# One-core gated cross-attention block: maxima of the first heads, weight preparation and token tiles moved to other steps

## What is computed

```python
x = x + tanh(g_xattn[0]) * mha(layernorm(x), ctx, ctx)        # 16 heads, causal from column 1089 on
h = layernorm(x)
# every row is scaled by its own maximum, then rounded to fp8
qx, sx = fp8_rows(h);  g = qx*sx @ (fp8_rows(Wgate)).T;  u = qx*sx @ (fp8_rows(Wup)).T
t = silu(g) * u                                               # 1408 hidden features
qt, st = fp8_rows(t);  y = qt*st @ (fp8_rows(Wdown)).T
x = x + tanh(g_ffn[0]) * y
```

## Time and profile before

| | us |
|---|---|
| median of 3 runs | 1055.09 |
| lowest, highest | 1054.97, 1057.81 |
| the profiled execution, own time | 1050.76 |
| its span in the trace | 1049.0 |
| PE, DVE, ACT, POOL busy | 952.6, 843.5, 684.4, 313.7 |

### The profile page before, as it was taken

One profiled execution on the slowest core, in us unless ns is written; L12 is line 12 of the kernel. 1 busy time (PEld: TensorE's weight loads), 2 busy tenths in 40 slices (PEclk: granted clock), 3 DMA queues, 4 the chain that ended last, 5 costly groups with the idle time before them and its releaser, 6 DMA issues.

```text
span 1049.0 us, 21140 instructions
## 1 busy us (share of the span) xinstructions
PE 952.6 (91%) x7706; PEld 396.1 (38%) x7706; DVE 843.5 (80%) x1438; ACT 684.4 (65%) x1420; POOL 313.7 (30%) x335
## 2 busy tenths in 40 slices
PE   3588899999999999999999999999999999989565
PEld 2223333333333434443434433444434343434333
DVE  7888988888987888787788979787888878645687
ACT  2047576777767776767667767777666766667544
POOL 3011333333321423232323324141323233334223
PEclk9999999999999999999999999999999999889889
DMA  6893342232792212123942221216832020000001
GB/s 135 124 215 93 78 118 67 67 95 62 166 125 55 81 46 60 43 64 92 127 85 58 59 72 33 69 38 137 116 61 64 11 48 27 1 11 2 11 2 41
DMA packets 157231, 74.89 MB, mean 71 GB/s; under 512 B 111096, under 2 KB 142920, under 8 KB 157128
## 3 DMA queue, kind: packets, MB, share of 16 engines
q1 hardware_dynamic: 155240, 67.70, 30.6%
q0 software_dynamic: 1760, 5.77, 2.1%
q10 hardware_dynamic: 128, 0.07, 0.0%
HBM read 43.28 MB, written 4.19 MB: 45 GB/s over the span
## 4 chain that ended last, share of the span: by engine, by line
PE 67%; DVE 18%; issue 7%; ACT 5%; POOL 2%; ACTq 0%; DVEq 0%; POOLq 0%
PE ps L963 22%; PE ps L937 14%; PE ps L880 8%; DVE mch L1193 7%; PE ps L984 6%; PE ps L1007 3%; PE ps L867 2%; PE ps L885 2%; ACT pr L692 2%; DVE ff L1100 1%; PE ps L906 1%; PE ps L943 1%; PE ps L918 1%; DVE ff L1093 1%; PE ps L908 1%
## 5 line engine op out<-in xcount | busy, mean ns | idle before, releaser
L692 ACT ACTIVATE pr<-ps 128x512 f32<-128x512 f32 (+4 forms) x832 | 398.3, 533 | 141.5 <-PE ps L937 84.3
L1193 DVE TENSOR_REDUCE mch<-ps 128x2 f32<-128x1024 f32 (+4 forms) x416 | 432.9, 1055 | 45.6 <-PE ps L885 23.4
L963 PE MATMUL ps<-pr,vf 128*33 128x512 f32 (+4 forms) x1664 | 378.3, 534 | 0.0
L937 PE MATMUL ps<-qst,kst 97*64 97x512 f16 (+4 forms) x1600 | 252.2, 371 | 12.7 <-ACT pr L692 9.2
L880 PE MATMUL ps<-kTh,qTh 32*128 32x512 f16 (+4 forms) x832 | 154.9, 370 | 21.9 <-DVE mch L1193 19.7
L880 PEld LDWEIGHTS ps<-kTh,qTh 32*128 32x128 f16 x832 | 39.6, 92 | 266.5 <-issue 115.2
L937 PEld LDWEIGHTS ps<-qst,kst 97*64 97x64 f16 (+1 forms) x1600 | 78.0, 110 | 106.3 <-ACT pr L692 67.4
L963 PEld LDWEIGHTS ps<-pr,vf 128*33 128x33 f32 (+1 forms) x1664 | 86.3, 112 | 55.1 <-issue 3.7
L1282 DVE SCALAR_TENSOR_TENSOR ff<-ps,scs,wsb 128x352 f32<-128x352 f32 x56 | 32.4, 582 | 56.0 <-PE ps L984 56.0
L984 PE MATMUL ps<-wgu,t_T 128*64 128x352 bf16 x768 | 66.5, 316 | 0.0
L486 POOL TENSOR_TENSOR ff<-ff,wsb 128x352 f32<-128x352 f32 x48 | 45.4, 946 | 67.0 <-DVE ff L1282 67.0
(11 more groups left out here) (157 smaller groups left out, 1163.4 us busy)
## 6 DMA issues: line engine op xcount, KB each, us to landing
kst<-kTh SPq DMA_DIRECT2D x128, 100.1 KB, 2.2
ksrc<-in_ctx SPq DMA_DIRECT2D x16, 768.0 KB
vf<-in_ctx SPq DMA_DIRECT2D x48, 256.0 KB, 5.6
kst<-kTl SPq DMA_DIRECT2D x64, 100.1 KB, 2.2
xs<-in_x SPq DMA_DIRECT2D x16, 256.0 KB, 4.1
qst<-qTh SPq DMA_DIRECT2D x128, 32.0 KB, 1.9
near<-in_ctx SPq DMA_DIRECT2D x4, 1024.0 KB, 7.8
out<-xs SPq DMA_DIRECT2D x16, 256.0 KB, 2.0
```

The lines of the kernel that those rows point to most:

```text
L692: nc.scalar.activation(pr[0:kn, n % NP, q0:S], ps[0:kn, j, q0:S], ACT.Exp, scale=SCALE).then_inc(ex_done, 1)
L937: last = nc.tensor.matmul(ps[a:e, j, q0:S], kst[s][0:ST, r, k0 + a:k0 + e], qst[s][0:ST, r, q0:S], start=True, stop=(t < DT))
L963: nc.tensor.matmul(ps[64 * j:64 * j + VW, 2 + pp % 2, q0:S], vf[0:kn, t, h, :], pr[0:kn, n % NP, q0:S], start=(t == 0), stop=(t == NT - 1) ...
L1193: nc.vector.tensor_reduce(mch[:, qt, 2 * hp:2 * hp + 2, c], both[:, :, 0:k1 - k0], AX.X, ALU.max).then_inc(dve_free, 1)
```

## The change

Six things are changed.

1. Only the first pair's 13 maxima jobs (`HALF`) of group 0 are made ahead of the loop, and its row of shifts is finished and sent alone (`first_finish`, `first_shift`). The other 13 jobs of group 0, all 26 of group 1 and 6 of group 2 are spread over the first 26 steps by `first_until`, up to two in one step.
2. Staging of group 0 uses PSUM banks of its own for three of its five parts (`FIRST_BANKS`), the gate matmul stands behind it on PE, ACT loads its function table with a dummy instruction, and the two memsets of 6404 ones both go to GpSimd behind `row_std`.
3. All weight blocks start 25 steps later, those of the down weight 9 steps apart and not 7.
4. The weight blocks are rounded in two passes on DVE (`round_negated`) from a size that ACT computes with an Abs pass; GpSimd's pass is gone.
5. The twelve tiles beside the attention all start 22 steps apart and end where they ended. Before, tiles 0 to 8 were 26 apart, each starting at u = 15, and only tiles 9 to 11 were 22 apart.
6. The statistics of the next x are four steps later, stores of finished tiles stand one group later in SyncE's order, and so do the loads of down weight blocks 2 and 3.

```diff
-    def max_job_at(at):
+    HALF = CH // PAIRS
+    FIRST = [(0, HALF + j) for j in range(HALF)] + [(1, j) for j in range(CH)] + [(2, j) for j in range(AHEAD)]
+    def first_until(at):
+        if at < 8:
+            return -(-HALF * (at + 1) // 8)
+        return HALF + -(-CH * (at - 7) // 15) if at < 23 else HALF + CH + 2 * (at - 22)
+    def max_jobs_at(at):
+        if at < STEPS:
+            return FIRST[first_until(at - 1) if at else 0:first_until(at)]
...
-    NORM_AT, X_STATS_AT, OUT_STATS_AT = (8, 9, 14, 16), (12, 13, 14, 15), (6, 7, 8, 9)
+    NORM_AT, X_STATS_AT, OUT_STATS_AT = (8, 9, 14, 16), (16, 17, 18, 20), (6, 7, 8, 9)
...
-        return STEPS * (n + NG) + 15 if n < TAIL - 3 else LAST - 1 - TILE_PERIOD * (TAIL - n)
+        return LAST - 1 - TILE_PERIOD * (TAIL - n)
...
-        return 1 + 7 * j if j < DC else 1 + 7 * DC + 19 * (j - DC) // 5
+        return 26 + 9 * j if j < DC else 26 + 9 * DC + 19 * (j - DC) // 5
...
+    FIRST_BANKS = {1: None, 2: None, 3: 1, 4: 0, 0: 2}
...
-        def weight_quant(pool, j):
-            rows, m, q = weight_job(j)
-            pool.wait_ge(w_added, j + 1)
-            if j >= 2:
-                pool.wait_ge(wT_mm, j - 1)
-            nc.gpsimd.tensor_tensor(q, rows, m, ALU.subtract).then_inc(wq_ready, 1)
...
+            act.wait_ge(wrow_used, j + 1)
+            if j >= 2:
+                act.wait_ge(wq_ready, j - 1)
+            nc.scalar.activation(m, rows, ACT.Abs, scale=SIZE_ROUND).then_inc(wrow_sized, 1)
...
+        def round_negated(dve, v, m, q, added, count, ready):
+            nc.vector.scalar_tensor_tensor(v, m, MIN_ROUND, v, ALU.max, ALU.add).then_inc(added, 1)
+            dve.wait_ge(added, count)
+            for sem_of, value in ready:
+                dve.wait_ge(sem_of, value)
+            return nc.vector.scalar_tensor_tensor(q, m, MIN_ROUND, v, ALU.max, ALU.subtract)
+
+        def weight_round(dve, j):
+            rows, m, q = weight_job(j)
+            dve.wait_ge(wrow_sized, j + 1)
+            round_negated(dve, rows, m, q, w_added, j + 1, [(wT_mm, j - 1)] if j >= 2 else []).then_inc(wq_ready, 1)
...
-            nc.gpsimd.memset(kst[0][ST - 1:ST, :, :], 1.0).then_inc(ones_in[0], 1)
-            pool.wait_ge(ones_in[0], 1)
             row_std(pool, 0)
-            masked_count(pool, 0)
+            pool.wait_ge(rstd_ready, 1)
+            for i in range(2):
+                nc.gpsimd.memset(kst[i][ST - 1:ST, :, :], 1.0).then_inc(ones_in[i], 1)
```

More of the change, by code:

```diff
@@ L143, in spare_bank, with numbered @@
         return 2 + (pp + 1) % 2
-    def numbered(*job, at=None):
-        one = spare_bank(at) if at is not None and fits_one_bank(job) else None
+    FIRST_BANKS = {1: None, 2: None, 3: 1, 4: 0, 0: 2}
+    def numbered(*job, at=None, alone=None):
+        one = spare_bank(at) if at is not None and fits_one_bank(job) else alone
         if one is not None and one in last_in:
@@ L150, in numbered @@
                 one = None
-        if one is not None:
+        if alone is not None:
+            banks[job] = one
+        elif one is not None:
             last_in[one] = (at, job)
@@ L166, in flamingo_gated_block @@
     for part in PARTS:
-        numbered("stage", 0, part)
-    for j in range(CH):
+        numbered("stage", 0, part, alone=FIRST_BANKS[part])
+    for j in range(HALF):
         numbered("max", 0, j)
-    numbered("shift", 0)
+    numbered("shift", 0, 0)
     for part in PARTS:
         numbered("stage", 1, part)
-    for j in range(AHEAD):
-        numbered("max", 1, j)
     for at in range(END):
@@ L178, in flamingo_gated_block @@
             before_values[(at - LAG) // NT] = latest.get(2 + (at - LAG) // NT % 2)
-        if max_job_at(at) is not None:
-            numbered("max", *max_job_at(at), at=at)
+        for job in max_jobs_at(at)[:1]:
+            numbered("max", *job, at=at)
         if gg + 2 < GALL and u in STAGE_AT:
@@ L184, in flamingo_gated_block @@
             numbered("turn", turned_at(at), at=at)
-        if gg < GALL and u == SUF_AT:
+        if gg < GALL and u == suf_at(gg):
             numbered("suf", gg, at=at)
-        if gg + 1 < GALL and u == MT_AT:
+        if at == 9:
+            numbered("shift", 0, 1, at=at)
+        if gg + 1 < GALL and u == shift_at(gg):
             numbered("shift", gg + 1, at=at)
+        for job in max_jobs_at(at)[1:]:
+            numbered("max", *job, at=at)
         for n, k in tiles_at(at):
@@ L455, in _ @@
                         load_values(sp, b + 1, t)
-            for n in range(GALL - NG - 1, TILES):
+            for n in range(GALL - NG - 2, TILES):
                 put_out(sp, n)
@@ L839, in free_slot @@
             elif before is None:
-                if banks[job] < 4:
+                if banks[job] < 4 and job[0] != "stage":
                     pe.wait_ge(ex_done, 2 * LAST)
@@ L887, in max_turn, with first_shift_turn @@
             last.then_inc(mx_mm, 1)
+        def first_shift_turn(pe, i):
+            job = ("shift", 0, i)
+            free_slot(pe, job)
+            pe.wait_ge(m_ready, i + 1)
+            for qt in range(QT):
+                last = nc.tensor.transpose(slot(job).bitcast(f16)[0:2, qt * P:(qt + 1) * P], m16[:, 0, qt, 2 * i:2 * i + 2], idh[:, :])
+            last.then_inc(mT_mm, 1)
         def shift_turn(pe, gg):
@@ L1037, in _ @@
                 gg, u = divmod(at, STEPS)
-                if max_job_at(at) is not None:
-                    max_turn(pe, *max_job_at(at))
+                for job in max_jobs_at(at)[:1]:
+                    max_turn(pe, *job)
                 if gg + 2 < GALL and u in STAGE_AT:
@@ L1366, in _ @@
                 gg, u = divmod(at, STEPS)
-                if gg + 1 < GALL and u == FINISH_AT:
+                if at == 8:
+                    first_finish(dve, s, 1)
+                if gg + 1 < GALL and u == finish_at(gg):
                     max_finish(dve, s, gg + 1)
-                if max_job_at(at) is not None:
-                    max_reduce(dve, *max_job_at(at))
+                for job in max_jobs_at(at)[:1]:
+                    max_reduce(dve, *job)
                 if gg + 2 < GALL and u in STAGE_AT:
```

139 lines of the change are left out of this document (76 added, 63 removed).

## The result

| | before | after |
|---|---|---|
| median of 4 runs, us | 1055.03 | 1101.07 |
| lowest, highest | 1054.89, 1057.81 | 1098.88, 1111.99 |
| span of the profiled execution | 1049.0 | 1097.1 |
| mean granted clock | 0.978 | 0.961 |

A forecast was written before the change was run, and what follows sets the result against it. PE was taken to set the pace in the loop, DVE ahead of it. Terms -10.3 + 3.4 - 6.0 + 5 + 4.4 + 20 = +16.5 us on 1055.1 gave 1071.6 us, eight-in-ten range 1042 to 1088.

The forecast's parts named there:

- Part 1: Way to the loop: first scores near 38 us, then PE waits about 14 us for group 2's keys; -9.2 us.
- Part 2: Rest of group 0: more maxima +5.7, slow clock +2.5, weight blocks gone -3.4, fewer waits -5.9; -10.3 us at its end.
- Part 3: Weights in groups 1 to 5: returning blocks +3.4, GpSimd's waits gone -6.0, extra ACT passes +5 and +4.4 us.
- Two-pass rounding: At weight blocks: PE's waits for GpSimd gone -6.0; ACT's extra pass +5 at large and +4.4 us at small blocks.
- Part 4: Tiles at 22 steps: eight new meetings of a down product with the next tile's rounding, 2.5 us each; +20 us.
- in the 2.5: Price in us of one down product meeting the next tile's rounding, said to include losing the hidden place at u = 15.
- The 3.0 us of a whole group: Cost of one meeting, from shift copies 61.6 against 56.1 us apart, less 2.5 for extra products.
- The test named in the prediction: Between 403 and 800 us: about 60.5 us from one shift copy to the next; under 58.5 would refute the tile term.
- the three: Rivals: meetings cost next to nothing, chance 0.20; group 2's keys not late, 0.10; ACT bound at the weights, 0.13.
- The first: Rival at tiles 0 to 8: meetings cost 0.5 us each, Abs passes hide more; 1048 us, chance 0.20.
- ACT at the weights: Rival at the small weight blocks: 0.7 us each instead of 0.2, +11, 1083 us; chance 0.13.

The follow-up runs named there:

- b_late22: b_tiles22 with the weight blocks at the changed kernel's steps and down weights 2 and 3 loaded one group later; ratio 1.0329 to the kernel before.
- b_round2: Kernel before with only the weights' rounding in two VectorE passes, one more ScalarE Abs pass and no GpSimd pass; ratio 1.0034, +3.6 us.
- b_tiles22: Kernel before with all twelve token tiles 22 steps apart and output stores one group later; ratio 1.0408, 1099.5 us.
- b_phase5: Kernel before with tiles 0 to 3 still 26 steps apart but starting at u = 5, and 22 apart from tile 4; ratio 1.0376, 1097.6 us.
- b_swap22: b_tiles22 with VectorE rounding the next tile's rows ahead of scaling the down product where both share a step; ratio 1.0236 to the kernel before, 1081.9 us.
- b_swap: Kernel before with only VectorE's order swapped: next tile's rounding ahead of scaling the down product; ratio 0.9948, 5.5 us faster.
- b_tiles24: Kernel before with tiles 0 to 7 24 steps apart, tile 8 at step 327, tiles 9 to 11 as before; ratio 1.0292, +31 us.
- b_spread5: b_phase5 with the second half of ScalarE's hidden scaling and its VectorE rounding one step later, for all tiles; ratio 1.0218 to the kernel before, 1082.1 us.

## Why the prediction was wrong

**Part 1 was right in its mechanism.** Forecast: keys in at 64.9 us, PE waits about 14 us. Measured: 64.81, and a wait of 10.29. PE came at 54.5 and not at 51. Scores of 4 x 512 took 1.05 to 1.07 us up to 49.92 and 0.62 at 52.72, so PE ran its first steps at the slow rate already; the forecast had put slow steps only behind the wait. (The granted clock of the profile reads 1.00 from 38 to 58 us, which these durations contradict.) The clock at 0.50 came as foreseen, from 58.16 to 68.40 us, most of it during the wait. Part 1 and 2 also said that the prologue alone nets little (-9.2 + 5.7 + 2.5 = -1.0); b_late22 reaches the end of group 0 within 0.5 us of the changed kernel with the old prologue.

**Part 2**: -10.3 forecast, -9.5 measured at the end of group 0. The shift row's copy came at 110.96 us, where the forecast named 105. That -10.3 and -9.5 agree within 1 us is partly luck: of the nine traces with the same code up to there, that of the kernel before is the earliest, and the others have their shift copy of group 0 2.6 to 6.6 us later.

**Part 3 was right in sum where it was measured.** Two-pass rounding: -6.0 + 5 + 4.4 = +3.4 forecast, +3.6 measured in b_round2, with the interval from +1.1 to +6.1. The weights' move: 9.3 us less in group 0 and 3.4 back later, so -5.9; b_late22 measured -8. Without the tiles the forecast was -3.5 us; the difference of the changed kernel and b_tiles22 is 0.18%, +2 us, with some 5 us of uncertainty. A few microseconds may be missing from the forecast here: prologue and rounding were to add -1.0 + 3.4 = +2.4 to b_late22 and added 10, with some 6 us of uncertainty. No run separates them.

**Part 4 failed: +20 forecast, +43 measured.** The step that failed is the sentence that the tiles' old place at u = 15, where ScalarE's two long passes (at u = 6 and 7, not 8) are hidden, is "in the 2.5" of a meeting. It is not: the place costs for each tile without any meeting (b_phase5: 5.1, 5.0, 1.7 and 7.2 us, of which the low clock makes 3.4, 3.4, 0 and 5.1). The meetings themselves were priced about right, as far as the swap shows it. b_swap22 gives 18 us for eleven of them, b_swap 5.5 for the three old ones, so the eight new ones make 12.5, or 1.6 each, where I took 2.5. The remaining 30 us, 3.8 for each of the eight tiles that were moved (tile 8 starts at step 327 in both kernels), had no term of their own. b_tiles24, with eight moved tiles and none of the new meetings, comes to about the same, 31. Spreading the burst took 5 us of the 30; for the rest it is open which work of the tiles stands badly.

The 3.0 us of a whole group seemed to bound everything that 22 steps bring. It could not, for the sampled group held no burst at a new place. Tile 8 starts at u = 15 as the others did, so its ScalarE passes stand at u = 6 and 7 of that group (814.64 to 818.81 us), and tile 9's at u = 2 and 3 of the next. In that group the swap takes off 2.4 us (61.6 to 59.2, the low clock behind the meeting included), and 0.6 is left. One sample was carried over to tiles whose costly work it did not contain. The test named in the prediction was also too mild: 60.5 us from one shift copy to the next was forecast, 64.7 and 66.2 came.

**The rivals.** None of the three was the case that came. The first was on the wrong side: it made the meetings cheap, and it too left out the place. ACT at the weights did not happen; ACT at the tiles did, and a rival of that kind was missing.

## What to carry to other kernels

Work that repeats beside a periodic loop has a place in the period as well as a density; before its spacing is changed, list what each of its long passes stands beside at every place that it will reach, and price the worst. Where the time of one sample is carried over, look whether the sample holds the very passes whose move is to be priced, and what else runs beside them. Where the clock makes single executions differ, compare a trace also with those of other kernels that share its code up to there. In an in-order queue put the work that others wait for ahead of work that itself waits: this one swap was worth 0.5% of the kernel before.

## What the runs showed of the hardware

A single wait of PE of 1.38 us in otherwise full work can have a fall of the granted clock behind it, and mostly had one here. b_phase5 has this wait five times, ended at 410.52, 471.71, 532.85, 592.41 and 656.15 us. Four of them had a stretch at 0.50 behind them, 0.8 to 2.0 us later and 6.83 or 10.24 us long; the third had none. At 6.83 us the clock's price, 3.4 us, is 2.5 times the wait's. In b_spread5 these five waits are gone, and with them the low stretches from 317.3 to 802.0 us, though waits of 1.63 and 1.68 us are left there (ended at 660.03 and 696.52). The 0.69 us wait at 506.48 us in b_swap22 had no low stretch behind it either.

So the same code does not always take the same time. Over nine traces with the same code up to step 118 the granted clock at 0.50 had cost between 1.7 and 15.4 us by step 101, and the copy of the shift row there came between 286.99 and 297.7 us.
